# Routing and plan of the transformer experts inside the stage of keys and values, keys in a ring of four PSUM banks

## The reference

```python
keys = x @ gate_Wk.T + gate_bk
scores = jnp.einsum('bsd,ed->bse', keys, expert_queries) * D ** (-0.5)
probs = jax.nn.softmax(scores, axis=-1)
_, idx = jax.lax.top_k(probs, K)                 # K = 2
mask = jax.nn.one_hot(idx, E).sum(-2)
gated = probs * mask
gated = gated / (gated.sum(-1, keepdims=True) + 1e-09)
...                                               # in each expert:
qkv = x @ Wqkv.T + bqkv                           # keys and values of all tokens
attn = softmax(q * scale @ k.T); ctx = attn @ v   # 8 heads of 32, then an FFN
```

## Time and profile before

| | |
|---|---|
| median of 3 runs | 3017.73 us (3017.52 to 3019.3) |
| profiled execution, its own time | 3008.34 us |
| its span in the trace | 3006.4 us |
| TensorE matmul busy | 2412.4 us (80%) |
| VectorE busy | 1548.0 us (51%) |
| ScalarE busy | 1158.1 us (39%) |
| mean granted TensorE clock | 0.898 of full |

### The profile page before, as it was taken

How to read it: one execution, slowest core, us unless ns; L and a number is a source line. 1 busy time by engine, 2 the same in 40 slices (tenths; PEclk the granted TensorE clock), 3 DMA queues, 4 the chain that set the end, 5 groups by cost and what they waited for, 6 DMA issues and landing times. The chain is left out here.

```text
span 3006.4 us, 52688 instructions
## 1 busy us (share of the span) xinstructions
PE 2412.4 (80%) x18555; PEld 2014.1 (67%) x18555; DVE 1548.0 (51%) x3102; ACT 1158.1 (39%) x2239; POOL 501.8 (17%) x812
## 2 busy tenths in 40 slices
PE   6989599769987859874976999999999999963266
PEld 4868499769965734764875777777777777753244
DVE  4646522232236651144445777777777777742455
ACT  3333222112213321122214666666666666624433
POOL 0000022112202100510001122222222222110043
PEclk9999699779988969976997999999999999976577
DMA  5000023134341121321665231335254452022144
GB/s 137 1 1 1 27 85 96 52 97 150 94 101 59 47 92 49 113 67 40 249 257 154 75 109 37 97 93 139 67 143 131 118 147 69 22 60 40 57 138 129
DMA packets 136391, 273.54 MB, mean 91 GB/s; under 512 B 33666, under 2 KB 70568, under 8 KB 133060
## 3 DMA queue, kind: packets, MB, share of 16 engines
q1 hardware_dynamic: 117332, 217.49, 23.2%
q0 software_dynamic: 18800, 52.69, 6.5%
HBM read 466.52 MB, written 65.74 MB: 177 GB/s over the span
## 5 line engine op out<-in xcount | busy, mean ns | idle before, releaser
L2245 PE MATMUL tx_ring<-g_ident,tx_p 128*128 128x128 f32 x2552 | 399.9, 284 | 40.9 <-DVE tx_p_t L2490 8.9
L2245 PEld LDWEIGHTS tx_ring<-g_ident,tx_p 128*128 128x128 f32 x2552 | 287.7, 142 | 147.3 <-DVE tx_p_t L2490 36.6
L2490 DVE COPY tx_p_t<-tx_ring 128x512 f32<-128x512 f32 x464 | 306.6, 686 | 147.3 <-PE tx_ring L2245 144.0
L2483 DVE TENSOR_REDUCE tx_neg_max<-tx_scores 128x1 f32<-128x1354 f32 x232 | 361.2, 1557 | 16.9 <-PE tx_scores L2233 16.7
L2379 ACT ACTIVATE tx_p<-tx_scores,tx_neg_max 128x1354 f32<-128x1354 f32 x232 | 322.6, 1390 | 104.2 <-DVE tx_neg_max L2483 103.9
L2233 PE MATMUL tx_scores<-tx_keys,tx_queries 96*128 96x512 f32 (+1 forms) x696 | 203.2, 401 | 14.5 <-DMA tx_queries<-tx_q_hi 11.2
L2386 ACT ACTIVATE tx_p_t<-tx_ring 128x384 f32<-128x384 f32 x232 | 113.4, 489 | 238.5 <-PE tx_ring L2245 235.3
L2285 PE MATMUL tx_ring<-tx_p_t,tx_values 128*32 128x128 f32 x5104 | 151.9, 274 | 17.4 <-ACT tx_p_t L2386 16.4
L2285 PEld LDWEIGHTS tx_ring<-tx_p_t,tx_values 128*32 128x32 f32 x5104 | 135.9, 110 | 28.3 <-ACT tx_p_t L2386 27.7
L2622 POOL TENSOR_SCALAR tx_std<-tx_mean_var 128x1 f32<-128x1 f32 x58 | 14.8, 256 | 769.5 <-DVE tx_mean_var L2554 403.0
L192 PE MATMUL ln_turned<-g_ident,g_xn 128*128 128x128 f32 x176 | 40.7, 419 | 117.8 <-DVE g_xn L179 117.8
(11 more groups left out here) (961 smaller groups left out, 5197.4 us busy)
## 6 DMA issues: line engine op xcount, KB each, us to landing
tx_keys<-expert_keys SPq DMA_DIRECT2D x696, 169.5 KB
lv1e_w<-in_L_ffn_W SPq DMA_DIRECT2D x232, 256.0 KB
tx_w<-in_L_ffn_W SPq DMA_DIRECT2D x58, 1024.0 KB
lv0e_w<-in_L_ffn_W SPq DMA_DIRECT2D x200, 256.0 KB
tx_values<-expert_values SPq DMA_DIRECT2D x58, 704.0 KB
tx_rows<-in_L_ffn_rows SPq DMA_DIRECT2D x29, 640.0 KB, 3.9
g_adj_t<-in_adj_t POOLq DMA_DIRECT2D x3, 3872.0 KB, 22.1
expert_values<-kv_v SPq DMA_DIRECT2D x8, 1408.0 KB
```

The lines of the kernel that those rows point to most:

```text
L2245: last = nc.tensor.transpose(ring[u % 2][:, (t - t0) * P:(t - t0 + 1) * P], p[n % 2][:, t * P:(t + 1) * P], g.ident[:])
L2483: nc.vector.tensor_reduce(neg_max[:, n % 4:n % 4 + 1], sc[n % 2][:, 0:N], AX_X, ALU.max, negate=True)\
L2490: nc.vector.tensor_copy(p_t[:, n % TURNED, t0:t0 + nt, :], ring[u % 2][:, 0:nt * P].rearrange("p (t q) -> p t q", q=P))\
```

## The change

The two blocks `ter` and `tep` go. Their work becomes a class `Sorting`, with a method for each piece, and is called from within `stage_keys_values`. VectorE's steps become a generator that stops (`yield`) after every instruction; `take` runs the next 12 of them at the head of each turn, before the turn's value blocks, up to the mark "rank" in turn 2 and up to the mark "found" in turn 5. So turns 0 and 1 take 12 each, turn 2 the remaining 2 of the routing and 5 of the plan, turns 3 and 4 take 12 each, turn 5 takes 11 and turn 6 the last 9. TensorE does `fold` and the logits ahead of turn 0, `rank` at the head of turn 3, the three parts of `turned` at the heads of turns 3, 4 and 5 (through one bank, each waiting for ScalarE's copy of the one before), and `found` at the head of turn 6. ScalarE does the exp ahead of turn 0's keys, the marks at the head of turn 5. GpSimd makes its constants at the block's start. SyncE issues the copy of `g.xn` first and the loads of the keys and values behind it; its completion is waited for at the block's end. `at_spot` is made in two halves.

The routing and the plan need two PSUM banks (`small`, `turned`). The keys' banks go from six to four: chunk u of all chunks goes to bank u mod 4, TensorE waits for `k_lo` of chunk u - 4, ScalarE's `k_hi` becomes three instructions of 452 columns, and VectorE's `k_lo` three of 452, one behind each of the turn's second, third and fourth value block. The DRAM writes of `k_hi` and `k_lo` stay one for each turn and wait for all three chunks. The other stages call the same helpers through `run`, which takes all steps at once; their instructions are unchanged.

```diff
 def softmax_to(link, nc, dve, values, probs, col, width, exp_asked, exp_done, n):
 
     link(nc.vector.tensor_reduce(col, values, AX_X, ALU.max))
+    yield
     nc.vector.tensor_tensor(probs, values, over(col, width), ALU.subtract).then_inc(exp_asked, 1)
+    yield
     dve.wait_ge(exp_done, n)
...
+        self.small, self.turned = s.ps("small", [P, BANK]), s.ps("turned", [plan.width, BANK])
...
+    def keep_rows(self, sync, src):
+        full = N // P
+        sync.dma_start(self.g.source_dram[0:full * P, :].rearrange("(b p) d -> p b d", p=P), src[:, 0:full, :])\
+            .then_inc(self.kept, 16)
+        sync.dma_start(self.g.source_dram[full * P:N, :], src[0:N - full * P, full, :]).then_inc(self.kept, 16)
...
+    def pe_rank(self, pe):
...
+        pe.wait_ge(self.shaped, 2)
+        pe.wait_ge(self.v_step, 1)
...
+    def pe_turn(self, pe, c):
...
+        pe.wait_ge(self.v_step, 1)
+        if c:
+            pe.wait_ge(self.turned_read, c)
...
+    def pe_found(self, pe):
...
+        pe.wait_ge(self.marked, 3)
+        pe.wait_ge(self.hot, 3)
+        for n in range(pairs):
...
+    def act_turn(self, act, c):
...
+        act.wait_ge(self.turned_full, c + 1)
...
+    def act_marks(self, act):
...
+        act.wait_ge(self.hot, 1)
+        act.wait_ge(self.v_step, 5)
...
+        for half in (slice(0, NB), slice(NB, pairs)):
+            nc.vector.tensor_tensor(at_spot[:, half, :],
+                                    spot[:].rearrange("p c b -> p (c b)")[:, half].unsqueeze(2).to_broadcast([P, NB, P]),
+                                    number_f[:].unsqueeze(1).to_broadcast([P, NB, P]), ALU.is_equal).then_inc(hot, 1)
+            yield
...
+    def dve_steps(self, dve):
+        yield from self.dve_route(dve)
+        yield from self.dve_plan(dve)
+
+
+def take(steps, count, marker=None):
+
+    n = 0
+    for at in steps:
+        if at is not None and at == marker:
+            return
+        n += 1
+        if marker is None and n >= count:
+            return
...
+KEY_BANKS = 4
+STEPS = 12
+RANK_AT, FOUND_AT, TURNS_AT = 3, 6, (3, 4, 5)
...
-        wide = [s.ps(f"wide{j}", [P, CH, BANK]) for j in range(KD)]
+        sort = Sorting(nc, g, s, *sorting, keys=keys)
+        wide = [s.ps(f"wide{u}", [P, BANK]) for u in range(KEY_BANKS)]
...
+            sort.keep_rows(sync, g.xn)
             sync.dma_start(bk[:], a["L2_ffn_bk"]).then_inc(bk_loaded, 16)
             load(0)
             load(1)
...
-                    sync.wait_ge(k_hi_done, KD * e + j + 1)
+                    sync.wait_ge(k_hi_done, CH * (KD * e + j + 1))
                     sync.dma_start(g.k_dram[e, 0, j * P:(j + 1) * P, :], k_hi[j][:].bitcast(F32)).then_inc(k_hi_kept[j], 16)
-                    sync.wait_ge(k_lo_done, KD * e + j + 1)
+                    sync.wait_ge(k_lo_done, CH * (KD * e + j + 1))
                     sync.dma_start(g.k_dram[e, 1, j * P:(j + 1) * P, :], k_lo[j][:].bitcast(F32)).then_inc(k_lo_kept[j], 16)
...
+            sort.rows_kept(sync, g.xn)
+
+        @block.gpsimd
+        def _(pool):
...
+            sort.pe_fold(pe)
+            sort.pe_logits(pe)
             for e in range(experts):
                 pe.wait_ge(w_lo_done, e + 1)
                 for j in range(KD):
-                    if e:
-                        pe.wait_ge(k_hi_done, KD * (e - 1) + j + 1)
-                        pe.wait_ge(k_lo_done, KD * (e - 1) + j + 1)
+                    turn = KD * e + j
+                    if turn == RANK_AT:
+                        sort.pe_rank(pe)
+                    if turn == FOUND_AT:
+                        sort.pe_found(pe)
+                    if turn in TURNS_AT:
+                        sort.pe_turn(pe, TURNS_AT.index(turn))
                     for c in range(CH):
+                        u = CH * turn + c
+                        if u >= KEY_BANKS:
+                            pe.wait_ge(k_lo_done, u - KEY_BANKS + 1)
                         if e + j == 0:
                             pe.wait_ge(x_lo_done, c + 1)
                         for k in range(KD):
-                            last = split_products(nc, wide[j][:, c, 0:CW],
+                            last = split_products(nc, wide[u % KEY_BANKS][:, 0:CW],
                                                   [part[e % 2][:, k, j * P:(j + 1) * P] for part in (w_hi, w_lo)],
                                                   [part[:, k, c * CW:(c + 1) * CW] for part in (x_hi, x_lo)],
                                                   k == 0, k == KD - 1)
-                    last.then_inc(k_full, 1)
+                        last.then_inc(k_full, 1)
...
+                    sort.act_fold(act)
                     weights_high(0)
             act.wait_ge(bk_loaded, 16)
+            sort.act_exp(act)
             for e in range(experts):
                 for j in range(KD):
+                    turn = KD * e + j
+                    if turn == FOUND_AT - 1:
+                        sort.act_marks(act)
+                    if turn - 1 in TURNS_AT:
+                        sort.act_turn(act, TURNS_AT.index(turn - 1))
                     if j and e + 1 < experts:
                         weights_high(e + 1)
-                    act.wait_ge(k_full, KD * e + j + 1)
                     if e:
                         act.wait_ge(k_hi_kept[j], 16 * e)
-                    nc.scalar.activation(k_hi[j][:].rearrange("p (c n) -> p c n", c=CH), wide[j][:, :, 0:CW], ACT.Identity,
-                                         bias=bk[:, KD * e + j:KD * e + j + 1]).then_inc(k_hi_done, 1)
+                    for c in range(CH):
+                        u = CH * turn + c
+                        act.wait_ge(k_full, u + 1)
+                        nc.scalar.activation(k_hi[j][:, c * CW:(c + 1) * CW], wide[u % KEY_BANKS][:, 0:CW], ACT.Identity,
+                                             bias=bk[:, KD * e + j:KD * e + j + 1]).then_inc(k_hi_done, 1)
 
...
+            steps = sort.dve_steps(dve)
+            sort.dve_widen(dve)
...
+                    turn = KD * e + j
+                    if turn == RANK_AT - 1:
+                        take(steps, 0, "rank")
+                    elif turn == FOUND_AT - 1:
+                        take(steps, 0, "found")
+                    elif turn == experts * KD - 2:
+                        take(steps, 1000)
+                    else:
+                        take(steps, STEPS)
+                    first = j * (NB // 2)
                     for b in (range(0, NB // 2), range(NB // 2, NB))[j]:
...
-                        if b == (1 if j == 0 else NB // 2 + 1):
-                            dve.wait_ge(k_hi_done, KD * e + j + 1)
-                            if e:
+                        c = b - first - 1
+                        if 0 <= c < CH:
+                            u = CH * turn + c
+                            dve.wait_ge(k_hi_done, u + 1)
+                            if e and c == 0:
                                 dve.wait_ge(k_lo_kept[j], 16 * e)
-                            nc.vector.scalar_tensor_tensor(out=k_lo[j][:].rearrange("p (c n) -> p c n", c=CH),
-                                                           in0=wide[j][:, :, 0:CW], scalar=bk[:, KD * e + j:KD * e + j + 1],
-                                                           in1=k_hi[j][:].rearrange("p (c n) -> p c n", c=CH),
+                            nc.vector.scalar_tensor_tensor(out=k_lo[j][:, c * CW:(c + 1) * CW], in0=wide[u % KEY_BANKS][:, 0:CW],
+                                                           scalar=bk[:, KD * e + j:KD * e + j + 1],
+                                                           in1=k_hi[j][:, c * CW:(c + 1) * CW],
                                                            op0=ALU.add, op1=ALU.subtract).then_inc(k_lo_done, 1)
...
-            stage_route(nc, g, "ter", g.xn_t, experts, "keys", weights, mask,
-                        keys=(held.tiles[1], held_bias), held=(held.tiles[0], held.loaded, None, 3))
-            stage_plan(nc, g, "tep", weights, mask[:], plan, coef=weights, src=g.xn)
-        stage_keys_values(nc, g, a, plan)
+            sorting = (plan, g.xn_t, experts, "keys", weights, mask[:], weights, (held.tiles[0], held.loaded, None, 3))
+            stage_keys_values(nc, g, a, plan, sorting, (held.tiles[1], held_bias))
```

More of the change, by code:

```diff
@@ L579, in divide_by_sum, with run @@
     link(nc.vector.tensor_reduce(col, values, AX_X, ALU.add))
+    yield
     if eps is not None:
         link(nc.vector.tensor_scalar(col, col, eps, None, ALU.add))
+        yield
     link(nc.vector.reciprocal(col, col))
+    yield
     link(nc.vector.tensor_tensor(values, values, over(col, width), ALU.mult))
+    yield
+def run(steps):
+    for _ in steps:
+        pass
 def stage_route(nc, g, tag, src_t, width, rule, weights, mask, held, keys=None):
@@ L653, in _ @@
                 link(nc.vector.tensor_tensor(chosen, chosen, other, ALU.add))
-                softmax_to(link, nc, dve, chosen, exps, c0, 4, exp_asked, exp_done, 1)
```

(24 more changed lines are left out.)

307 lines of the change are left out of this document (added).

## The result

Four runs of the kernel before had a median of 3017.6 us (3015.1 to 3019.3), four of the changed kernel 2977.4 us (2976.3 to 2982.8). The ratio is 0.9871, with a 95% interval of 0.9854 to 0.9888. That is 38.9 us less by the ratio, which goes by the means, and 40.2 by the two medians. The forecast was 2978.7 us, for a difference of 39.0.

What follows compares the result with a forecast made beforehand. Bounds: a single 47.5 us chain from layer norm to first key matmul, then TensorE's waits for VectorE's value evacuation. -33.9 - 13.4 + 7.3 + 1.0 = -39.0 us off the 3017.7 median gives 2978.7 us, range 2969 to 2995.

Steps and rivals of the forecast that it cites:

- Part 1, the chain ahead of the keys: Before the first key matmul: keys start once logits and first weights are through, no longer behind the plan; 33.9 us gained.
- Part 2, the ring: Keys' stage: `k_lo` chunks behind three value blocks shorten each pair of turns by 1.67 us, 13.4 us over 8 pairs.
- The recurrence over banks and back-to-back starts: Keys' stage: model of when value blocks are ready and VectorE starts them; pair 17.72 us before, 16.03 after.
- Part 3, the added work: Keys' stage turns: TensorE's sorting matmuls and VectorE's steps not hidden add 7.3 us, bounds 2.7 and 28.4.
- the late weights: Turn 3: expert 2's weights arrive late and, with VectorE's steps, delay the value blocks; +1.4 us.
- TensorE's own work: Turns with sorting: `rank`, `turned` and `found` take 0.7, 1.4 and 1.1 us at full clock, 3.2 in all.
- The sum's nothing for VectorE's steps in this turn: Turn 0: keys take 5.3 us at the low clock, so steps end before the first value block; cost 0.
- Part 4, the end: End of the keys' stage: the last `k_lo` is written right ahead of `v`; +1.0 us, bounds 0 and 1.7.
- The later weights: Six odd turns: weights come two microseconds later still, about +1.5 us each, 2988 us; chance 0.20.
- The ring without effect: Keys' stage: the stall stays at 1.2 us a turn despite the shorter chunks, 2992 us; chance 0.08.
- the unhidden steps: Keys' stage: VectorE's 23 us of steps delay the values one for one, 2995 us; chance 0.07.
- The clock's fall: From turn 4: idle gaps keep the clock at half, each turn about 7.3 us longer, about 3066 us; chance 0.03.

Runs made afterwards that it cites:

- e9: The changed kernel with the first expert's weights loaded ahead of the copy of `g.xn`; one execution, 2952.5 us against 2986.4 for the kernel before.
- e1: The kernel before with only the ring of four key banks by chunk, sorting left in its own blocks; 2971.8 us against 2982.3, ratio 0.9962.
- e2: The changed kernel with all three `k_lo` chunks behind the turn's second value block; 2960.9 us against 2982.3, ratio 0.9923.
- e3: The changed kernel with three PSUM banks for values and three for keys, instead of two and four; 2943.8 us, ratio 0.987.
- e4: The changed kernel with the load of `w` for expert e + 2 issued at expert e's head, before its keys' writes; 2944.3 us, ratio 0.987.
- e7: e6 with VectorE's steps spread over the turns by their length instead of twelve by twelve, `found` at turn 7; 2959.5 us, ratio 0.9835.
- e6: The changed kernel with the edits of e3 and e4 together: three value banks, three key banks, weights loaded early; 2962.2 us, ratio 0.9835.
- e8: The changed kernel with 24 steps at a turn's head for 12, `rank` at turn 2, `found` at turn 4; one execution, 2978.5 us against 3010.7.
- e5: The changed kernel once more without an edit, on another chip; 2970.8 us against 3010.7 for the kernel before, ratio 0.9866.

## Why the prediction was right, step by step

- **Part 1, the chain ahead of the keys.** Predicted -33.9, measured -33.5. The start was read off as the later of logits and weights. The first key was forecast 12.4 us behind A (1392.6 - 1380.25) and came at 12.8. Behind A the logits ended at 12.4, 0.6 later than in before, and the weights' split last, at 12.7. Of the two orders that the earlier trace rows left open, e9 shows the one in which the copy comes first: moved behind the weights, it gave them back 6.6 us, as long as SyncE had waited for it (6.5). By the Trainium skill, "DMA: Bandwidth & Descriptors", "Queues, rings and completion order", each DMA engine consumes its descriptors in ring order. The order of the two runs agrees: 10.4 us behind the copy, 3.8 ahead of it.
- **Part 2, the ring.** Predicted -13.4, measured 8 x 1.67 = 13.4 by the quiet pairs, in e1 without the other parts. The recurrence over banks and back-to-back starts also forecast e2 (18.2, measured 18.20) and e3 (15.3, measured 15.30), so the cause is shown, not only the size. The Trainium skill, "VectorE: DVE Perf Modes", "The DRAIN you can't avoid", was read in the prediction as whole durations one behind the other, which would have made the pair 16.5 us; it was 16.03, and starts 0.08 us ahead of the last one's end are in the timeline above. The reading was too narrow: the same paragraph ends by saying that a next operation that is not held starts earlier, and these rows agree with that.
- **Part 3, the added work.** Predicted +7.3, measured +8.1 over the first turns (each from the first value of a turn to that of the next, less the same in a quiet turn: 0.6, 0, 2.3, 2.5, 1.7, 1.0). Up to the first value of turn 4 it is 5.4 for 5.8; what follows, up to that of turn 6, is 2.7 for the 1.5 of turns 5 and 6. Within this, e4 shows the late weights to be 1.43 for 1.4, and e7 TensorE's own work, the part that no placing can hide, 2.65 for 3.2. The size that was off is turn 5's: I took TensorE's work at the full clock, but behind the 2.04 us gap of turn 4 its last values and the `turned` and first keys of turn 5 ran for 3.3 us at 0.50, and `turned` took 0.84 us for a planned 0.4. Half of 3.3 is 1.7 us, enough for the 1.2. That it is the cause isn't shown by an experiment that changes the clock alone. For it speaks e6, with the same steps in each turn: its gap is 1.55 us, the clock stays at 1.00, and from the first value of turn 4 to that of turn 5 it takes 7.29 us, just as long as in a quiet turn. But e6 has a third value bank as well:

```profile
1426.00:1429.00 3.00, 1.45 (x13) 1.25 (x12) 2.93 (x6) 2.45 (x4) 0.00 (x0) 1.00 0.68 173
1429.00:1432.00 3.00, 3.00 (x21) 2.85 (x22) 3.00 (x8) 0.00 (x0) 0.00 (x0) 1.00 0.94 367
```

- **The first turn** is where a microsecond went that the sum left at nothing: its first value came 7.25 us behind the first key, for 6.25 before. It goes with the moment at which the granted clock rises from 0.50 to 1.00, in tenths of a microsecond behind the first key: at 3.2 in before and in e9 (6.25 and 6.19 us), at 5.4 with the change (7.25), at 5.9 in e1 (7.44), at 6.0 in e7 (7.47). As e1 has the old head and is among the late ones, and e9 has the new head and the ring and is as early as before, neither part makes it late by itself; with one profile of before, more isn't shown. The sum's nothing for VectorE's steps in this turn held only because the keys were slow: they end 6.8 us behind the first key. In e4, where the clock rises at 3.0 and the keys are as fast as in before, the first value waits for them and comes at 6.84. In the profile after, over the time ahead of the keys and over this turn:

```profile
1377.24:1390.04 12.80, 11.57 (x56) 11.44 (x56) 2.81 (x4) 3.61 (x5) 2.83 (x31) 0.55 0.66 212
1390.04:1396.38 6.34, 6.34 (x19) 5.61 (x20) 4.34 (x13) 2.99 (x5) 0.00 (x0) 0.57 0.01 3
```

- **Part 4, the end.** Predicted +1.0, measured +0.97; SyncE waited 5.1 us for the write of `v`, 4.1 before:

```profile
SPq L2295 <- DMA expert_values<-kv_v: 5.1, 1, 5.1
```

- **The rivals.** The later weights: the quiet odd turns show no cost (`w_lo` ends at 1476.53, and the first block is ready at 1477.00). The prediction's sign for them, long waits of `w_lo` for `w_hi`, did come (8.8 us for 1.0, longest 2.0) and misled: VectorE has 0.47 us left there, and e4, without these waits, has the same pair. The ring without effect falls with e1, and the unhidden steps with the 8.1 us measured for 23 of steps. The clock's fall was half right: it came behind the gap of turn 4, and in e8 for longer, but it was back at 1.00 some 4.6 us behind the gap's end, and 4.3 in e8, and did not spread from turn to turn. Its price was at most 1.7 us (3.3 us of work at 0.50), and not 7 in every turn.
- **The whole.** Between the marks 36.8 less, for 39.0: 1.0 is the first turn's, 0.8 the added work's, 0.4 the head's. That the whole times differ by 39 to 40 all the same is inside their interval of 5 us each way; the forecast was right to about 2 us, and its closer hit is luck.

## What to carry to other kernels

When an engine that works in order evacuates a small ring of banks, count when each bank comes free: the same work cut into pieces and put between the evacuations can take a whole stall away (17.70 to 16.03 us a pair), while the same pieces in one place take away nothing (18.20). Steps that are to be hidden beside another engine's work should be placed by their length against the time that each turn hides, not by an equal number, and the loads issued behind that stage's writes should be looked at again, since a faster stage meets them earlier. Where whole times vary by some microseconds and by chip, let a pair of marks around the change carry the verdict.

## What the runs showed of the hardware

The last experts' stage (`nee_row`), with the same instructions, takes some 20 us more on one chip than on another: 71 to 74 us in e1 to e4, which ran on one, 91 to 92 in e5 to e8 on the other. In e3's kernel and in e5's (duration min/median/max in ns, first and last start in us):

```profile
L3240 PE MATMUL nee_row<-nee_w,nee_h x116: 378/380/635, 2827.9 to 2900.0; 128*128 128x256 f32 x116
```

```profile
L3240 PE MATMUL nee_row<-nee_w,nee_h x116: 379/379/795, 2844.1 to 2935.7; 128*128 128x256 f32 x116
```

Windows over the two, e3's first:

```profile
2828.00:2900.00 72.00, 61.46 (x385) 51.37 (x385) 51.15 (x160) 44.37 (x136) 45.14 (x47) 0.99 0.54 161
```

```profile
2844.00:2935.70 91.70, 70.06 (x386) 58.22 (x385) 51.32 (x160) 45.84 (x138) 45.79 (x48) 0.89 0.41 129
```

The granted clock is 0.99 in the one and 0.89 in the other, with VectorE and ScalarE as busy in both; 8.6 us of the difference are longer matmuls, 11.1 idle time. Which came first, the waits or the lower clock, was not tried.

TensorE works 11.6 of the 12.8 us ahead of the first key, nearly all of it matmuls of 8 columns, at a granted clock of 0.55; the keys' first turn, busy without a gap, still has 0.57 (0.50 for 5.4 us, then 1.00). I had counted on the lower clock, but not that it would last longer than in before, where the logits end 34 us ahead of the first key.

Inside the stage the clock fell to 0.50 behind gaps of 2.03 or 2.04 us in the change and in e2, e4, e5 and e9, behind one of 2.57 in e3 and within one of 4.72 in e8. It stayed at 1.00 behind 1.55 us in e6 and behind 2.50 in e8.
